# Projections placed evenly over the pairs, and VectorE's emptying of a PSUM item bank moved behind the product of its pair

## Chip, core and metric

One NeuronCore of a Trainium2 chip runs the whole program. The metric is device time in microseconds, the median of three runs. Engines: TensorE (PE), VectorE (DVE), ScalarE (ACT), GpSimd (POOL), and SyncE (SP), whose queue issues every DMA of this kernel.

## What is computed

Input x is (2, 2048, 512). In short:

```python
h = x @ cond_W[id] + cond_b[id]                 # per batch element
q, k, v = split(h @ w_qkv.T)                    # 16 heads of 32
s = causal(q @ k.T / sqrt(32) - slope*|i-j|)
p = 0.5 * (1 + s * rsqrt(1 + s*s));  p /= sum(p) + 1e-6
x1 = x + (p @ v) @ w_out.T
z = layernorm(x1 + relu(x1 @ W1[l] + b1) @ W2[l] + b2) * gamma + beta
out = x1 + int8_linear(z, w8)                   # one scale over all of z
```

The softmax is a rational one: no maximum is taken, and each score s becomes 1 + s/sqrt(1+s²) by elementwise passes.

## The kernel before

**Groups, chunks, pairs.** Attention is done for four heads at a time: 2 batch elements by 4 head groups are 8 groups, G = 0 to 7. A group walks over four chunks c of 512 queries, and within a chunk over the key blocks. Its unit of work is a *pair*: 128 keys by up to 2 x 512 scores, in one of two PSUM slots of `sc`. A group has 68 pairs; chunks begin at pairs 0, 5, 18 and 39 (`first`), and the last five pairs of each chunk lie on the diagonal, with masks added by further small matmuls (L920).

**What a pair costs each engine.** PE makes the scores (L917). ACT squares them (L748), takes the reciprocal root (L750), and later squares 1+g for pair k-2 (L713). DVE multiplies scores and root, the *product* (L1135, `s_g`), and then adds for pair k-2, the *numerator* (L1066, `s_num`). POOL squares y (L674). PE's matmul for pair k+2 needs the slot that the product of pair k frees. Six pairs later PE multiplies the results with v and with ones (L896, the *pv* step, into `ov` and `dn`, for two pairs at a time). At a chunk's last pv step DVE empties `ov` and `dn` (L1079 and L1080; L1180 and L1181 for a chunk of the group before), SP moves the denominators (L532), DVE inverts them (L1084), SP moves them back (L538, L540), and DVE multiplies (L1090, the *divide*). The next chunk's first pv step waits for the emptying (`s_out`).

**Items.** All other PE work is cut into *items* of one or four parts, put between the matmuls of pairs. An item writes one of two banks of `it` and is then emptied, so item i waits until item i-2 has been emptied, and some wait for their own inputs as well (`needs`). Kinds: the projections q, k, v of a chunk of 512 tokens, four parts each (L817, and L821 for v); `xt` and `h`, the conditional linear layer of 128 tokens (L801, L834); `o`, `rt`, `a`, `w2`, `zt`, the output projection, adapter and norm of 128 tokens (L841, L801, L848, L850, L801). DVE empties q, k (L993 and L995, through `stage`), v (L985), xt (L998), h (L1001), o (L1005) and w2 (L1008); ACT empties rt, a and zt. A projection's name with "next" belongs to the group after.

**Who runs items.** Group 0 (`opening`) has projections and 12 tiles of xt and h; groups 1, 2, 5, 6 (`plain`) have 12 projections and nothing else; group 3 (`closing`) adds 16 tiles of xt and h for batch element 1; group 4 (`joining`) adds 16 tiles of o to zt; group 7 (`ending`) has 10 of those and no next group.

**What sets the order.** `Group.__init__` (L108) writes out one list of events, which every engine's program follows: "qk" for pair k, then item parts, then "pv". It keeps a budget `left`, which grows by 1.61 us + `slack` for each pair and shrinks by the cost of a part (0.86 for a projection part). A job may begin from pair `start`, goes at once at pair `end` whatever the budget, and waits `lag` pairs behind the jobs it follows. In DVE's program (`group`, L1092) the product and numerator of pair k are written by `scored(k)`. Before the change that call is held back until the next "pv" or "qk":

```python
for e in g.events:
    if e[0] in ("qk", "pv") and k is not None:
        scored(k)
        k = None
    if e[0] == "qk":
        k = e[1]
    elif e[0] == "item":
        ... empty_item(...)
```

so an item that ends in pair k is emptied in front of the product of pair k, whenever PE has made it.

**SP's order.** For each q or k item SP waits for the emptying and issues 13 DMAs (`operand`, L473 twelve times and L474), which bring the chunk's rows of `stage` to `qmv` or `kst`. PE waits for them (`s_op`) before the chunk's first scores. The queue is one line: the denominators (L532) and the loads of x tiles (L461, L465) stand in it by the event list. At the start of `closing` SP waits until *all* items of the group before have been emptied (`sp.wait_ge(s_evac, dve_base)`), then issues the conditional weights (L478, L480) and two x tiles (L461). At the start of `joining` and `ending` it waits likewise and then issues seven loads of weights (L484) and two x tiles (L465). In `closing` the first xt item stands at pair 2 and waits for its x tile; in `joining` the first o item stands at pair 1 and waits for all seven loads (`s_bw`).

Before the change q of chunk 1 is an item at pair 0 of its own group; v and k of chunk 1 are both items of pair 61 of the group before.

## Time and profile before

| | |
|---|---|
| median of 3 runs | 2234.24 us (2229.65 to 2236.6) |
| the profiled execution: its own time | 2231.39 us |
| its span in the profile | 2229.5 us |
| granted TensorE clock, mean | 0.922 of full |
| busy: PE, DVE, ACT, POOL | 1768.5, 1805.8, 1713.3, 1691.9 us (79, 81, 77, 76% of the span) |
| DVE product L1135, numerator L1066 | 544 each; 662.4 and 773.9 us |
| ACT L748, L750, L713 | 544 each; 551.6, 575.5, 566.2 us |
| ACT idle before L748, of it until PE sc L917 | 310.8 us, 185.6 us |
| DMA | 138.49 MB, mean 62 GB/s |

Busy times are unions of an engine's instructions. The idle time of a group is that of its engine just before those instructions, with what ended it. Four engines lie within five points of each other, so shares don't tell what bounds; the order of waits does. The profiled execution is 2.9 us under the median; a profile covers one execution, so sums are made against its 2231.39 us.

### The profile page before, as it was taken

Reading aid. Unit: us, or ns where it says so; the run is one execution under the profiler, and the core shown is the slowest. Engines: PE = TensorE matmul, PEld = TensorE weight load, DVE = VectorE, ACT = ScalarE, POOL = GpSimd, SP = SyncE. Lnnn points to the kernel's source line nnn. Section 1 sums busy time; section 2 is a strip of 40 time slices with the busy share of each in tenths; the row PEclk is TensorE's granted clock in tenths of the full one; section 3 lists DMA queues with packets and bytes.
Section 4 is the critical chain, followed back from the end, with each engine's and each line's share of the span. In section 5 each row is a group of like instructions: output and inputs, shape, how many; then the busy total and the mean of one; then the engine's idle time right before and its main releaser. Section 6 shows DMA issues by size and latency. Waiting matters only on the chain.

```text
span 2229.5 us, 29232 instructions
## 1 busy us (share of the span) xinstructions
PE 1768.5 (79%) x10640; PEld 897.9 (40%) x10640; DVE 1805.8 (81%) x1730; ACT 1713.3 (77%) x1842; POOL 1691.9 (76%) x720
## 2 busy tenths in 40 slices
PE   5668877777787789999987888886887687897765
PEld 4554433333333336565443443332333233443331
DVE  4238888988889889889785878888889888998838
ACT  0037998889888988878775878898889888897652
POOL 2027888888888887778775877888888888897738
PEclk9899989988988899999998998998999899999889
DMA  5411101110111022211323121210112012222146
GB/s 179 148 49 45 49 21 45 40 49 20 45 41 49 21 68 74 68 34 40 97 63 92 43 77 40 50 54 16 35 47 58 15 46 76 52 61 60 46 165 207
DMA packets 126602, 138.49 MB, mean 62 GB/s; under 512 B 27868, under 2 KB 78044, under 8 KB 126044
## 3 DMA queue, kind: packets, MB, share of 16 engines
q1 hardware_dynamic: 126460, 136.64, 21.6%
q8 instruction: 84, 1.38, 0.3%
q14 instruction: 58, 0.48, 0.1%
HBM read 54.02 MB, written 22.80 MB: 34 GB/s over the span
## 4 chain that ended last, share of the span: by engine, by line
PE 38%; DVE 21%; ACT 21%; issue 11%; POOL 4%; SPq 3%; DMA 2%; DVEq 0%; POOLq 0%; ACTq 0%
ACT yb L748 8%; DVE gb L1135 7%; DVE gb L1066 7%; PE sc L917 7%; ACT gb L713 6%; PE it L817 6%; PE ov L896 6%; ACT yb L750 5%; PE dn L896 5%; PE it L834 4%; PE it L841 3%; PE it L821 3%; SPq L473 3%; POOL oT L707 2%; DMA area<-in_x_dram 1%
## 5 line engine op out<-in xcount | busy, mean ns | idle before, releaser
L674 POOL TENSOR_TENSOR yb<-yb 128x1024 f32<-128x1024 f32 x544 | 1503.0, 2776 | 432.6 <-DVE gb L1135 415.0
L748 ACT ACTIVATE yb<-sc 128x1024 f32<-128x1024 f32 x544 | 551.6, 1014 | 310.8 <-PE sc L917 185.6
L1135 DVE TENSOR_TENSOR gb<-sc,yb 128x1024 f32<-128x1024 f32 x544 | 662.4, 1218 | 142.8 <-ACT yb L750 139.1
L1066 DVE TENSOR_TENSOR gb<-gb,yb 128x1024 f32<-128x1024 f32 x544 | 773.9, 1423 | 0.1
L917 PE MATMUL sc<-qmv,kst 128*128 128x512 f32 (+3 forms) x1280 | 482.8, 461 | 263.0 <-DVE gb L1135 250.5
L750 ACT ACTIVATE yb<-yb 128x1024 f32<-128x1024 f32 x544 | 575.5, 1058 | 17.2
L713 ACT ACTIVATE gb<-gb 128x1024 f32<-128x1024 f32 x544 | 566.2, 1041 | 0.0
L917 PEld LDWEIGHTS sc<-qmv,kst 128*128 128x128 f32 x1280 | 231.5, 202 | 568.1 <-DVE gb L1135 412.0
L896 PE MATMUL ov<-gb,vv 128*32 128x512 f32 (+3 forms) x2560 | 326.4, 594 | 29.5 <-DVE den L1080 24.6
L896 PE MATMUL dn<-gb,ones 128*32 128x512 f32 (+3 forms) x2560 | 312.5, 572 | 0.0
L817 PE MATMUL it<-hT,wT 128*128 128x512 f32 x496 | 245.2, 627 | 8.2 <-ACT area L728 3.2
L896 PEld LDWEIGHTS dn<-gb,ones 128*32 128x32 f32 x2560 | 88.7, 119 | 178.1 <-issue 172.6
L834 PE MATMUL it<-area 128*128 128x128 f32 x1024 | 134.4, 291 | 26.6 <-DVE area L998 22.8
L834 PEld LDWEIGHTS it<-area 128*128 128x128 f32 x1024 | 131.0, 206 | 34.0 <-DVE area L998 27.1
L817 PEld LDWEIGHTS it<-hT,wT 128*128 128x128 f32 x496 | 98.5, 202 | 95.6 <-issue 77.6
L841 PE MATMUL it<-area,oT 128*128 128x512 f32 x224 | 115.0, 646 | 15.6 <-DVE oT L1090 7.4
L821 PE MATMUL it<-wT,hT 128*128 128x128 f32 x992 | 123.1, 278 | 0.7 <-DVE hT L1001 0.5
L821 PEld LDWEIGHTS it<-wT,hT 128*128 128x128 f32 x992 | 120.4, 194 | 6.2 <-DVE area L1008 1.0
L896 PEld LDWEIGHTS ov<-gb,vv 128*32 128x32 f32 x2560 | 56.1, 113 | 156.5 <-issue 96.5
L920 PE MATMUL sc<-unseen,ident 128*128 128x128 bf16 x512 | 116.5, 238 | 0.0
L993 DVE TENSOR_SCALAR stage<-it 128x512 fp32r<-128x512 f32 x64 | 43.6, 681 | 63.6 <-PE it L817 50.5
L801 PE MATMUL it<-ident,area 128*128 128x128 f32 x336 | 53.4, 292 | 43.0 <-POOL area L665 14.4
(113 smaller groups left out, 1086.9 us busy)
## 6 DMA issues: line engine op xcount, KB each, us to landing
qmv<-stage SPq DMA_DIRECT2D x384, 64.0 KB
kst<-stage SPq DMA_DIRECT2D x384, 64.0 KB
area<-in_x_dram SPq DMA_DIRECT2D x58, 256.0 KB, 2.8
out_dram<-oT SPq DMA_DIRECT2D x32, 256.0 KB, 3.2
den<-rec_d SPq DMA_DIRECT2D x31, 256.0 KB
wT<-wT_d SPq DMA_DIRECT2D x7, 768.0 KB, 4.4
x_d<-area SPq DMA_DIRECT2D x16, 256.0 KB, 2.6
z_d<-area SPq DMA_DIRECT2D x16, 256.0 KB, 2.7
```

The source lines that it names most:

```text
L674: pool.tensor_tensor(y, y, y, ALU.mult).then_inc(s_y2, 1)
L713: act.activation(gview(n), gview(n), ACT.Square, bias=1.0).then_inc(s_g2, 1)
L748: act.activation(yview(n), sc[:, n % SLOTS], ACT.Square).then_inc(s_s2, 1)
L750: act.activation(yview(n), yview(n), ACT.Abs_reciprocal_sqrt, bias=1.0).then_inc(s_y, 1)
L817: r = pe.matmul(bank, wT[:, "qk".index(what), part, :], hT[:, part, c * CH:(c + 1) * CH], **ends)
L821: r = pe.matmul(bank[:, part * P:(part + 1) * P], hT[:, k, tok], wT[:, 2, k, :], start=(k == 0), stop=(k == KC - 1))
L834: r = pe.matmul(bank[:, part * P:(part + 1) * P], wc[:, k, part * P:(part + 1) * P], xT[:, a, k, :], start=(k == 0), stop=(k == KC - 1))
L841: r = pe.matmul(bank, oT[:, part, tok], woT[:, part, :], **ends)
L896: r = pe.matmul(dst[p.head * D:(p.head + 1) * D, p.q0:p.q0 + p.width], lhsT, gview(n)[:, p.bank, p.at:p.at + p.width], start=(p.kb == 0), ...
L917: r = pe.matmul(out, kst[:, p.head, p.kb * P:(p.kb + 1) * P], qmv[:, c % 2, p.head, p.q0:p.q0 + p.width], start=True, stop=not diagonal)
L1066: dve.tensor_tensor(gview(n), gview(n), yview(n), ALU.add).then_inc(s_num, 1)
L1135: dve.tensor_tensor(gview(n), sc[:, n % SLOTS], yview(n), ALU.mult).then_inc(s_g, 1)
```

## The change

It does five things. (1) The list of projections is written out with a start and an end for each; q of chunk 1 becomes an item of the group before (`("q", 1, "next")`, from pair 63, placed between pairs 64 and 67), and k and v of chunk 1 are no longer in one pair. (2) The budget of a pair becomes 0.9 + slack, with every group's own slack raised by 0.7, so that it stays the same in the four other groups and falls from 1.61 to 0.9 in `plain`. (3) DVE writes `scored(k)` at the "qk" event, so an item that ends in pair k is emptied behind product, numerator, inversion and divide of pair k. (4) SP waits for the group's last scores before it issues the 13 DMAs of the moved q, since they overwrite the slot of `qmv` that chunk 3 uses. (5) The numbering of banks and the waits for them are carried over the border of groups, since the number of items is odd in some.

```diff
--- before.py
+++ after.py
@@ -138,22 +138,21 @@
                 made.setdefault((job.name[1] // TT, 0 in chunks), []).append(job)
-        projections = []
-        for c in range(n_chunks):
-            p0, p1 = self.first[c], self.last[c]
-            if c < n_chunks - 1:
-                whats = "qkv" if c or opens else "q"
-                for what in whats:
-                    lag = 0 if what == "q" or c == 0 else STAGED
-                    after = [] if what == "q" else [projections[-1]] if what == "k" else []
-                    projections.append(Job((what, c + 1), [0.86] * 4, made.get((c + 1, False), []) + after,
-                                           p0 + (2 if c else 0), p1 - (6 if c else 4) + (4 if what == "v" else 0), lag or EVAC))
-            elif has_next:
-                for what, nxt, start in (("q", 0, 2), ("v", 0, 2 * TT + LAG), ("k", 0, 2 * TT + 2),
-                                         ("v", 1, 4 * TT + LAG), ("k", 1, 4 * TT + 2)):
-                    after = [projections[-2]] if what == "k" else []
-                    projections.append(Job((what, nxt, "next"), [0.86] * 4, made.get((nxt, True), []) + after,
-                                           p0 + start, p1 - 6, STAGED if what == "k" else EVAC))
+        f, end = self.first, len(self.pairs) - 1
+        over = [f[3] + 2 * TT * (c + 1) for c in range(2)]
+        wanted = [(("q", 1), 0, 0), (("k", 1), 0, 8), (("v", 1), 0, 13)] if opens else []
+        wanted += [(("q", 2), f[1] + 1, f[2] - 5), (("k", 2), f[1] + 2, f[2] + 8), (("v", 2), f[1] + 3, f[2] + 10),
+                   (("q", 3), f[2] + 1, f[3] - 5), (("k", 3), f[2] + 2, f[3] - 3), (("v", 3), f[2] + 3, f[3])]
+        if has_next:
+            wanted += [(("q", 0, "next"), f[3] + 1, f[3] + 16), (("k", 0, "next"), over[0] + 1, end - 8),
+                       (("v", 0, "next"), over[0] + LAG, end - 6), (("k", 1, "next"), over[1] + 1, end - 4),
+                       (("v", 1, "next"), over[1] + LAG, end - 2), (("q", 1, "next"), end - 4, end)]
+        projections, staged = [], None
+        for name, start, until in wanted:
+            after = made.get((name[1], len(name) == 3), []) + ([staged] if name[0] != "v" and staged else [])
+            projections.append(Job(name, [0.86] * 4, after, start, until, EVAC if name[0] == "v" or not staged else STAGED))
+            if name[0] != "v":
+                staged = projections[-1]
         tracks = [[job for job in others if job.name[1] % 2 == 0], [job for job in others if job.name[1] % 2], projections]
         self.events, current, part, left, order = [], None, 0, 0.0, []
         n_pairs, n_units = len(self.pairs), len(self.units)
@@ -165,7 +164,7 @@
         for k in range(n_pairs):
             self.events.append(("qk", k))
-            left = max(-1.0, min(left, 0.5)) + 6 * CH / 1200 - 0.95 + slack
+            left = max(-1.0, min(left, 0.5)) + 0.9 + slack
             while True:
                 if current is None:
                     ready = [t for t in tracks if t and t[0].start <= k and
@@ -193,7 +192,6 @@
         self.items = [job for job in order if job.parts]
         self.operands = [job.name for job in self.items if job.name[0] in ("q", "k")]
         self.ranks, self.evacs = ranks(self.items)
-        assert not has_next or len(self.items) % BANKS == 0 and all(eng == "dve" for eng, _ in self.ranks[-BANKS:])
     def item(self, *name):
         return [job.name for job in self.items].index(name)
@@ -216,10 +214,10 @@
     first = plain.first + [len(plain.pairs)]
     opening = Group(NC, [job for j in range(TT, KB)
-                         for job in cond_jobs(j, first[j // TT - 1], first[j // TT] - (12 if j >= 2 * TT else 5))], True, True, 0.8)
+                         for job in cond_jobs(j, first[j // TT - 1], first[j // TT] - (12 if j >= 2 * TT else 5))], True, True, 1.5)
     closing = Group(NC, [job for j in range(KB)
-                         for job in cond_jobs(j, 2 if j < TT else first[j // TT] + 1, first[NC] - 24 + j)], True, slack=0.0)
+                         for job in cond_jobs(j, 2 if j < TT else first[j // TT] + 1, first[NC] - 24 + j)], True, slack=0.7)
     def joined(j):
@@ -228,12 +226,12 @@
         return after_jobs(j, 1 if c < NC - 1 else LAG + 10, min(over - 3 if i < 2 else over, first[NC] - 1),
                           min(over - 1 if i < 2 else over + 8, first[NC] - 1))
-    joining = Group(NC, [job for j in range(KB) for job in joined(j)], True, slack=0.8)
+    joining = Group(NC, [job for j in range(KB) for job in joined(j)], True, slack=1.5)
     assert all(job.at <= first[job.name[1] // TT + 1] + LAG - 2 for job in joining.items if job.name[0] == "o")
     DONE = KB - TT - 2
     ending = Group(NC, [job for j in range(DONE) for job in
-                        after_jobs(j, first[j // TT + 1] + LAG + 2 * NORM_LAG + 3, first[NC] - 9 + j - KB + TT, first[NC] - 1)], False, slack=0.3)
+                        after_jobs(j, first[j // TT + 1] + LAG + 2 * NORM_LAG + 3, first[NC] - 9 + j - KB + TT, first[NC] - 1)], False, slack=1.0)
     UNITS, PAIRS = len(plain.units), len(plain.pairs)
     TOTAL = B * NG * PAIRS
@@ -447,7 +445,7 @@
         def ops_before(g, G):
-            return 2 if g is opening else 2 * NC * G + 3
+            return 2 if g is opening else 2 * NC * G + 4
         def zs_before(b, j):
@@ -588,6 +586,8 @@
                     if what in ("q", "k"):
                         sp.wait_ge(s_evac, dve_base + rank)
                         nhg = hg if len(e[1].name) == 2 else (0 if g is closing else hg + 1)
+                        if e[1].name == ("q", 1, "next"):
+                            sp.wait_ge(s_qk, (G + 1) * PAIRS)
                         operand("qk".index(what), c, nhg)
                     elif what == "v" and c == NC - 1 and g.has_next:
                         sp.wait_ge(s_item, base + item + 1)
@@ -781,10 +781,12 @@
         def _(pe):
             pe.wait_ge(s_const, 2)
-            def emptied(i, of, dve_base, act_base):
-
-                if i < 0:
+            def emptied(i, of, dve_base, act_base, before=None):
+
+                if i < 0 and before is None:
                     pe.wait_ge(s_evac, dve_base + i + 1)
+                elif i < 0:
+                    emptied(len(before.items) + i, before.ranks, dve_base - before.evacs["dve"], act_base - before.evacs["act"])
                 elif of[i][0] == "dve":
                     pe.wait_ge(s_evac, dve_base + of[i][1])
                 else:
@@ -909,7 +911,7 @@
                             pe.wait_ge(s_g, n - SLOTS + 1)
                         for what, at in (("q", g.first[c]), ("k", g.first[c] + 2 * TT * c)):
                             if k == at:
-                                own = g.operands.index((what, c)) + 1 if (what, c) in g.operands else -(c == 0 and carry)
+                                own = g.operands.index((what, c)) + 1 if (what, c) in g.operands else -2 * (c == 0 and carry)
                                 pe.wait_ge(s_op, 16 * NPROJ * (ops_before(g, G) + own))
                         for p in g.pairs[k]:
                             out = slot[:, p.bank, p.at:p.at + p.width]
@@ -922,10 +924,10 @@
                     elif e[0] == "part":
                         d = b + (1 if g is closing else -1 if g is joining else 0)
                         if e[2] == 0:
-                            emptied(item - BANKS, g.ranks, dve_base, act_base)
+                            emptied(item - BANKS, g.ranks, dve_base, act_base, before[0])
                             if g is opening and e[1].name == ("q", 1):
                                 pe.wait_ge(s_wt, 16)
-                        r = compute(it[:, (PRO + item) % BANKS], e[1], e[2], d, G + 1 if len(e[1].name) == 3 else G,
+                        r = compute(it[:, (base + item) % BANKS], e[1], e[2], d, G + 1 if len(e[1].name) == 3 else G,
                                     g.ranks, dve_base, act_base)
                     elif e[0] == "item":
                         r.then_inc(s_item, 1)
@@ -941,8 +943,10 @@
                             own = c >= 2 or c and not carry
                             pe.wait_ge(s_evac, dve_base + (g.ranks[g.item("v", c)][1] if own else 0))
                         products(G, g, u)
+                before[0] = g
             pe.wait_ge(s_const, 9)
+            before = [None]
             for_groups(group)
             for u in plain.late:
                 products(B * NG, plain, u)
@@ -1115,7 +1119,7 @@
                     if len(name) == 3:
                         v_free = G * UNITS + units_over(c)
                         k_free = G * PAIRS + pairs_over(c)
-                        q_free = G * PAIRS + last
+                        q_free = G * PAIRS + last if c == 0 else None
                     elif what in ("q", "k", "v"):
                         if carry:
                             v_free = (G - 1) * UNITS + units_over(c)
@@ -1124,7 +1128,7 @@
                             q_free = G * PAIRS + g.first[c - 1]
                         elif carry:
                             q_free = G * PAIRS
-                    empty(name, d, base + item, dve_base + g.ranks[item][1], ops_before(g, G) + his, v_free, q_free, k_free, (PRO + item) % BANKS)
+                    empty(name, d, base + item, dve_base + g.ranks[item][1], ops_before(g, G) + his, v_free, q_free, k_free, (base + item) % BANKS)
                 def scored(k):
@@ -1146,11 +1150,9 @@
                 k = None
                 for e in g.events:
-                    if e[0] in ("qk", "pv") and k is not None:
-                        scored(k)
-                        k = None
                     if e[0] == "qk":
                         k = e[1]
+                        scored(k)
                     elif e[0] == "item":
                         eng, rank = g.ranks[item]
                         if eng == "dve":
@@ -1169,8 +1171,6 @@
                                 output(G, hg, g, u, c, g is opening and c == 0)
                             else:
                                 output_prev(G, prev_hg, u, c)
-                if k is not None:
-                    scored(k)
                 for late in reduced:
                     largest(*late[1:])
```

## Rows read from the trace of the kernel before

**Rows 1.** Busy time by stretch: groups 2, 3, 4, 7 and 0

```profile
core 0: us, PE busy (x) PEld busy (x) DVE busy (x) ACT busy (x) POOL busy (x), PEclk, DMA share, GB/s
...
600.30:825.70 225.40, 176.11 (x1057) 77.87 (x1056) 198.18 (x173) 200.50 (x206) 191.56 (x69) 0.90 0.17 45
825.70:1066.50 240.80, 225.59 (x1635) 142.27 (x1634) 213.60 (x205) 202.21 (x205) 191.43 (x69) 0.98 0.22 61
1066.50:1395.00 328.50, 273.71 (x1470) 136.79 (x1469) 248.06 (x269) 238.13 (x301) 238.19 (x133) 0.93 0.23 63
...
1846.20:2102.50 256.30, 213.87 (x1253) 100.73 (x1251) 227.01 (x226) 223.06 (x266) 220.23 (x109) 0.94 0.18 50
91.00:375.20 284.20, 225.08 (x1448) 134.19 (x1447) 205.47 (x191) 200.41 (x203) 186.49 (x67) 0.93 0.16 41
```

**Rows 2.** Timeline, two pairs of group 2 with no items

```profile
729.84 1.23 DVE L1135 TENSOR_TENSOR gb<-sc,yb 128x1024 f32<-128x1024 f32 x1 [0.59 <-ACT yb L750]
730.59 1.00 ACT L748 ACTIVATE yb<-sc 128x1024 f32<-128x1024 f32 x1
730.98 1.22 DVE L1066 TENSOR_TENSOR gb<-gb,yb 128x1024 f32<-128x1024 f32 x1
...
731.12 0.74 PE L917 MATMUL sc<-qmv,kst 128*128 128x512 f32 x2 [0.36 <-DVE gb L1135]
...
733.54 1.00 ACT L748 ACTIVATE yb<-sc 128x1024 f32<-128x1024 f32 x1
```

**Rows 3.** Timeline, DVE and ACT, pairs 0 and 1 of group 2

```profile
602.36 0.69 DVE L993 TENSOR_SCALAR stage<-it 128x512 fp32r<-128x512 f32 x1 [0.43 <-PE it L817]
...
605.14 1.02 ACT L748 ACTIVATE yb<-sc 128x1024 f32<-128x1024 f32 x1 [1.77 <-PE sc L920]
```

**Rows 4.** Timeline, PE, DVE and ACT, pair 61 of group 2

```profile
802.64 3.60 PE L817 MATMUL it<-hT,wT 128*128 128x512 f32 x8
...
806.28 0.69 DVE L993 TENSOR_SCALAR stage<-it 128x512 fp32r<-128x512 f32 x1 [2.74 <-PE it L817]
...
806.81 1.02 ACT L748 ACTIVATE yb<-sc 128x1024 f32<-128x1024 f32 x1 [2.85 <-PE sc L917]
```

**Rows 5.** Timeline, PE, pair 20 of group 2

```profile
665.97 3.27 PE L817 MATMUL it<-hT,wT 128*128 128x512 f32 x4
```

**Rows 6.** Timeline, PE and ACT, pair 12 of group 2

```profile
642.14 1.93 PE L896 MATMUL ov<-gb,vv 128*32 128x512 f32 x8 [2.71 <-DVE den L1080]
...
646.36 1.02 ACT L748 ACTIVATE yb<-sc 128x1024 f32<-128x1024 f32 x1 [4.50 <-PE sc L920]
```

**Rows 7.** Timeline, SP and DVE, pairs 25 to 29 of group 2

```profile
687.78 7.48 SPq L473 DMA_DIRECT2D kst<-stage  x12
...
698.47 0.25 DVE L1084 RECIPROCAL rec<-rec 128x16 f32<-128x16 f32 x1 [2.76 <-DMA rec<-den]
```

**Rows 8.** Timeline, PE, ACT: group 0 pair 20; group 3 pair 43

```profile
215.21 3.47 PE L834 MATMUL it<-area 128*128 128x128 f32 x16 [3.80 <-DVE hT L1001]
...
221.30 1.02 ACT L748 ACTIVATE yb<-sc 128x1024 f32<-128x1024 f32 x1 [8.05 <-PE sc L917]
...
987.23 1.02 ACT L748 ACTIVATE yb<-sc 128x1024 f32<-128x1024 f32 x1 [4.71 <-PE sc L917]
```

**Rows 9.** Timeline, SP, ends of groups 2 and 3

```profile
815.95 0.44 SPq L478 DMA_DIRECT2D area<-in_L_cond_W_dram  x1
...
817.03 1.29 SPq L461 DMA_DIRECT2D area<-in_x_dram  x2
...
1056.68 0.35 SPq L484 DMA_DIRECT2D area<-woT_d  x1
...
1060.49 0.38 SPq L484 DMA_DIRECT2D bet<-in_L_cond_beta_dram  x1
```

**Rows 10.** DMA issues: KB each, median us from issue to landing

```profile
area<-in_x_dram SPq DMA_DIRECT2D x58, 256.0 KB, 2.8
...
area<-in_L_cond_W_dram SPq DMA_DIRECT2D x2, 1024.0 KB, 5.5
```

## The prediction, made before the change was run

> **What bounds the kernel now.** The four engines' busy shares are too close to name one, so I first read busy time by stretch, a stretch being a group from its first L748 to the next group's [rows 1]. A plain group lasts 225.4 us and ACT is busy for 200.5 of it; closing lasts 240.8, joining 328.5, ending 256.3, opening 284.2, while ACT's work hardly grows (202 in closing) and PE's does (226 and 274). Then I read the timeline where a plain group has no items: one square (L748) starts 2.95 us after the other, with no idle time on ACT, while DVE waits 0.59 before each product and PE waits for the slot [rows 2]. So undisturbed pairs are bound by ACT, 68 x 2.95 = 200.6 us a group, and a plain group loses 24.8 us to stalls. That the reader is to see: time is lost only where ACT waits before L748, nearly always because PE brought the scores late.
>
> In group 2 three of these waits are large. After pair 0, PE is in four parts of q: ACT idles 1.77 [rows 3]. In pair 61, v and k together: PE computes k until 806.2, DVE stands 2.74 before emptying it, ACT idles 2.85 [rows 4]. At pair 12, DVE is late with emptying `ov` and `dn` (a divide is in front), PE waits 2.71 for it, then its pv matmuls run slowly, ACT idles 4.50 [rows 6]. The other 24.8 - 1.8 - 2.9 - 4.6 = 15.5 us are shorter waits of the same kinds, one of them behind a 2.76 us wait of DVE for denominators, whose L532 stands in SP's queue behind the 13 DMAs of k3 [rows 7].
>
> **Where the items go.** I followed the planner's arithmetic (budget, starts, ends, lags) for both versions. In plain, items that took two pairs take three (2, 1, 1 parts), k1 is at pairs 56 to 59, v1 at 61 to 63, q1 at 64 to 67. In the other groups the budget is the same, and mostly the projections' places change. I counted how often an item needs a bank or an input that DVE empties from an item of the same pair or the one before. Plain: never, in either version. Same pair: closing 2 before, 3 after; joining 7 and 12; ending 1 and 0; opening, without pair 0, 7 and 8. Pair before: about 70 in both.
>
> **Term 1, plain groups, four times.** Gone: pair 0 (1.8) and pair 61 (2.9) [rows 3, 4]. The inversion's wait: k3 now ends at pair 26, behind SP's L532 of that pair, not before it; of 2.76 us on DVE some 1.1 reached ACT, since product and numerator (1.14 us each by their starts [rows 2]) leave 0.59 + the PE's lead. Two projection parts with a pv step took PE too long where the clock was low: 3.27 us for four matmuls, where eight took 3.60 [rows 4, 5]; one part there saves about 0.6 at four places, 2.4. Returned: the diagonal pairs 63 to 67 now hold six parts at 0.9 (a quarter of 3.60), with about 1 us uncovered. Pair 12 stays: the divide and `s_out` are not touched. Emptying behind the numerator holds up the next product by 2 x 1.14 + 1.4 - 2.95 = 0.7, under the PE's lead, which is 733.54 - 731.12 - 0.74 = 1.7; if the clock is low that cover is 1.2. Sum 1.8 + 2.9 + 1.1 + 2.4 - 1 = 7.2, times 4: **-29** (bounds -12: pairs 0 and 61 alone, with what the tail gives back; -52: half of the 24.8).
>
> **Term 2, SP's queue at two borders.** The moved q is the last item, and its 13 DMAs now stand in front of the next group's loads; the loads also wait for its emptying. Closing: emptying ends some 3.5 us after the first square, as now [rows 3]; 13 DMAs take 8.0 (7.48 and one of about 0.5 [rows 7]); the x tile is issued 1.1 after the weights [rows 9] and lands in 2.8 [rows 10]: 3.5 + 8.0 + 1.1 + 2.8 = 15.4. PE stands at xt of pair 2 until then, then has two xt (1.1), a pv step in low clock (3.2), scores (1.2): square 3 at 20.9, not 3 x 2.95 = 8.9: +12. Now these loads go out at 816 to 818 [rows 9], 8 us before the group. Joining: emptying ends near the first square (the item is at pair 66), 8.0, 3.8 from first to last weight [rows 9], landing 5.5 (the median of a weight tile [rows 10]) = 17.5; o needs all seven; three parts (4) and scores (1.2) put square 2 at 22.7 where two pairs and the q gave 7: +16. Ending needs its weights at pair 20: covered. SP's new wait for the group's last scores costs nothing: they are issued before the item's emptying ends. The moved q's own DMAs land at 3.5 + 8.0 + 2.8 = 14.3 after the first square in plain, and pair 5's scores are wanted near 5 x 2.95 - 0.8 = 13.9; that is where the same 13 DMAs land now, so again nothing. Together **+28** (20 to 32).
> The page DMA: Bandwidth & Descriptors of the Trainium skill (Rules for kernel authors) says to issue a DMA early and wait late; the change does the reverse here, and no row prices that other than as above.
>
> **Term 3, waits for a bank inside a pair or from the pair before.** An item that ended in pair k was emptied as soon as PE was done. Now the emptying waits for scores (0.74), square and root (2.0), product and numerator (2.3): some 5 us after the pair's scores start, 6 with its own 0.7, while PE reaches the dependent item after 2. PE executes in order, so pv of k and scores of k+1 stand behind it. Before has two places where an emptying was late like this: behind a numerator and a divide PE waited 3.80 and ACT then idled 8.05; behind a numerator alone ACT idled 4.71 [rows 8]. A same-pair need thus costs between 0 (PE far ahead) and 8; I take 4, nearer to the row without a divide. There are 17 such pairs (the chain in opening's pair 6 counted once): 68, less 25 for waits those places have already. The other side of this edit is that a product no longer stands behind an unfinished item; in pairs 0 and 61 of plain that is in term 1, and in closing and joining PE is by then behind with the next scores, so the earlier product frees a slot, and a square of POOL's, that nobody waits for yet: nothing, at best some of the 25 us. A need from the pair before is mostly covered by a pv step: 0 to 2, I take 0.5, some 50 times: 25. **+68** (5 to 142).
>
> **Term 4, pairs 0 and 61 in the others.** Pair 0 three times 1.8, pair 61 three times 2.9, less 1 for each tail: **-12** (-15 to -9). In opening's pair 0 the first xt is emptied 6 us later (root and product of pair 0 come first), and k1 leaves the chain, worth as much: 0. **Term 5:** in closing, joining and ending k3 stays ahead of L532 and is emptied 2.3 later, so DVE waits longer for the inversion: **+3** (0 to 6).
>
> Sum: -29 + 28 + 68 - 12 + 3 = **+58**, against the profiled execution's 2231.4 (span 2229.5 and 1.9 around it): 2289; the median of the runs lies 2.9 higher, so 2292.
>
> **Rivals.**
> *A, the two banks cover it.* If PE is far enough ahead, term 3 is near 0 and -29 + 28 - 12 + 3 leaves -10: 2224. It decides where term 3 stays under 4. For it: PE is idle 20% in plain. Against: it is busy for 226 of 240.8 us in closing [rows 1]. The Trainium skill's page Perfetto Trace Analysis (Matmuls) has independent matmul groups rotate through PSUM banks so that emptying one overlaps the next one's matmuls; by it this rival would win.
> *B, the clock.* Spread parts leave PE less busy at a stretch, and plain is already at 0.90 [rows 1]. A part at low clock is 3.27 / 2 - 3.60 / 4 = 0.73 dearer [rows 4, 5]; 48 parts, a third of it uncovered, 12 us a group: 58 + 48, 2340. Against: closing is at 0.98 with spread items.
> The same page (Matmul Optimizations) says that it matters that matmuls run back to back in batches; the rows of low clock here follow PE's waits, as it would have it.
> *C, plain gains almost nothing*, as the tail on the diagonal gives back pairs 0 and 61 and the rest is `s_out`: term 1 is -5: 2316.
> *D, the terms cancel:* 2235.
>
> **Chances.** Forecast 0.50, A 0.20, B 0.10, C 0.12, D 0.08. 0.3% (6.7 us) is about what a measurement can tell from no change. Faster 0.20, same 0.08, slower 0.72. The range: term 3 alone gives 2229 to 2366 with the others kept; I cut it to 2220 to 2350, which takes in A, B, C and D and leaves out the ends of two terms together.
>
> **What would show it.** Right: plain stretches near 218; in closing ACT idle some 12 us before square 3, with PE waiting for area<-in_x_dram, in joining 16 before square 2; PE's waits for DVE's emptying lines (L998, L1001, L1005, L993, L1008) grow by tens of us in sum. L1084 no longer waits in plain. Wrong: if PE's waits for emptied banks don't grow, A holds; if the granted clock in plain falls below 0.88, B. A plain group above 222 is C. If closing and joining start without a wait for DMA, term 2 fails.

## The result and the profile after

| | before | after |
|---|---|---|
| median | 2234.47 us (4 runs, 2229.65 to 2236.6) | 2396.72 us (4 runs, 2388.09 to 2398.59) |
| profiled execution: own time, span | 2231.39, 2229.5 us | 2398.59, 2396.7 us |
| granted clock, mean | 0.922 | 0.893 |

The ratio is 1.0724, with an interval of 1.0704 to 1.0744. The kernel became slower by 162 us. The prediction said slower, by 58, in a range that ended at 2350: the sign is right, the size is not, and the result lies outside the range.

The first view is busy time by stretch, of the kernel after: groups 1, 2 (both plain), 3 (closing), 4 (joining), 7 (ending) and 0 (opening), the stretches of [rows 1] and one plain group more:

```profile
core 0: us, PE busy (x) PEld busy (x) DVE busy (x) ACT busy (x) POOL busy (x), PEclk, DMA share, GB/s
387.90:603.80 215.90, 173.17 (x1060) 76.73 (x1056) 196.60 (x171) 200.03 (x206) 191.57 (x69) 0.92 0.15 39
603.80:819.00 215.20, 171.85 (x1060) 75.84 (x1056) 199.24 (x173) 200.09 (x206) 191.64 (x69) 0.93 0.16 40
819.00:1107.20 288.20, 235.84 (x1636) 146.78 (x1632) 211.84 (x207) 202.28 (x206) 191.48 (x69) 0.91 0.18 49
1107.20:1541.40 434.20, 306.41 (x1472) 155.12 (x1472) 237.61 (x269) 240.02 (x301) 221.26 (x132) 0.83 0.19 54
...
1972.60:2269.70 297.10, 225.54 (x1236) 105.11 (x1232) 221.45 (x226) 224.35 (x266) 213.70 (x109) 0.89 0.18 51
91.90:387.90 296.00, 235.30 (x1468) 138.84 (x1468) 200.74 (x194) 200.76 (x204) 186.12 (x67) 0.90 0.15 40
```

A plain group takes 215 to 216 us where it took 225.4, and its clock rose from 0.90 to 0.93. Everything else grew: opening by 11.8, closing by 47.4, joining by 105.7, ending by 40.8 us. ACT's and DVE's work in these stretches is what it was to within 12 us. In joining PE's busy time rose from 273.7 to 306.4 us for the same work (1470 and 1472 matmuls recorded), at a granted clock of 0.83 in place of 0.93.

Where the time stands idle, from the costliest groups of instructions of the page after:

```profile
L1139 DVE TENSOR_TENSOR gb<-sc,yb 128x1024 f32<-128x1024 f32 x544 | 663.0, 1219 | 436.2 <-ACT yb L750 433.3
L748 ACT ACTIVATE yb<-sc 128x1024 f32<-128x1024 f32 x544 | 550.7, 1012 | 445.0 <-PE sc L919 248.1
```

ACT's idle time before the square grew from 310.8 to 445.0 us, DVE's before the product from 142.8 to 436.2. DVE waits for ACT's root, ACT for PE's scores; what PE waits for closes the ring. PE's rows in the view of waits after:

```profile
PE sc L919 <- DVE gb L1139: 202.0, 169, 4.8
PE it L836 <- DVE area L1002: 36.5, 11, 11.3
...
PE it L803 <- DMA area<-in_x_dram: 26.7, 4, 12.4
...
PE it L843 <- DVE area L1009: 19.9, 5, 5.0
PE it L803 <- DVE hT L1005: 18.5, 6, 6.0
PE it L850 <- DVE area L1009: 15.6, 7, 4.2
PE it L803 <- DVE vv L989: 14.7, 4, 7.5
```

The columns are the sum, the number of waits and the longest. The first row is PE's wait for a slot of `sc`; it was 250.5 us before, so it is not what grew. Summed over all rows of this view in which PE waits for one of DVE's emptying lines, it is 51.5 us in 35 waits before and 181.9 us in 62 waits after.

Lengths of all groups, from a group's first L748 to the next group's (ending: to 3.4 us behind its own last), in us; worked out from the starts of L748 in each trace. The kernels below the first two are the experiments that follow.

| kernel | opening | plain | plain | closing | joining | plain | plain | ending |
|---|---|---|---|---|---|---|---|---|
| before | 284.2 | 225.1 | 225.3 | 240.9 | 328.5 | 225.9 | 225.3 | 256.3 |
| after | 296.0 | 215.9 | 215.2 | 288.2 | 434.2 | 216.0 | 215.2 | 297.1 |
| after, emptying in front again | 277.5 | 215.0 | 215.2 | 251.1 | 361.7 | 216.1 | 215.5 | 258.5 |
| before, emptying behind | 303.4 | 230.3 | 231.1 | 286.2 | 387.3 | 231.1 | 229.7 | 304.2 |
| after, loads first | 295.1 | 215.9 | 215.2 | 274.6 | 424.0 | 215.9 | 215.4 | 300.3 |
| after, emptying between | 298.9 | 222.1 | 225.6 | 277.8 | 401.1 | 223.3 | 225.3 | 275.3 |
| front and loads first | 275.6 | 215.1 | 215.2 | 239.9 | 348.8 | 213.1 | 214.8 | 259.3 |

### The profile page after: what moved, and what is told of

Same layout as the page of the kernel before. It is cut to its first block, busy times and chain, and to the rows that moved or that the text cites. A ratio compares the mean times of both kernels' runs of the same rounds, so it can differ in the third digit from the quotient of the medians.

```text
span 2396.7 us, 29236 instructions
## 1 busy us (share of the span) xinstructions
PE 1819.2 (76%) x10637; PEld 924.9 (39%) x10640; DVE 1781.9 (74%) x1730; ACT 1715.3 (72%) x1842; POOL 1668.4 (70%) x720
## 3 DMA queue, kind: packets, MB, share of 16 engines
q1 hardware_dynamic: 126460, 136.64, 20.3%
## 4 chain that ended last, share of the span: by engine, by line
PE 33%; ACT 27%; DVE 17%; issue 10%; POOL 6%; SPq 3%; DMA 3%; DVEq 0%; POOLq 0%; ACTq 0%
ACT yb L748 11%; ACT yb L750 8%; ACT gb L713 8%; DVE gb L1070 6%; PE sc L919 6%; PE ov L898 6%; DVE gb L1139 5%; PE dn L898 5%; PE it L843 4%; PE it L836 4%; PE it L819 4%; POOL yb L674 3%; SPq L471 3%; POOL oT L707 2%; PE it L823 1%
## 5 line engine op out<-in xcount | busy, mean ns | idle before, releaser
L674 POOL TENSOR_TENSOR yb<-yb 128x1024 f32<-128x1024 f32 x544 | 1494.6, 2759 | 495.1 <-DVE gb L1139 479.3
L1139 DVE TENSOR_TENSOR gb<-sc,yb 128x1024 f32<-128x1024 f32 x544 | 663.0, 1219 | 436.2 <-ACT yb L750 433.3
L748 ACT ACTIVATE yb<-sc 128x1024 f32<-128x1024 f32 x544 | 550.7, 1012 | 445.0 <-PE sc L919 248.1
L1070 DVE TENSOR_TENSOR gb<-gb,yb 128x1024 f32<-128x1024 f32 x544 | 758.2, 1394 | 3.6 <-POOL yb L674 3.6
L919 PE MATMUL sc<-qmv,kst 128*128 128x512 f32 (+3 forms) x1280 | 489.3, 467 | 215.2 <-DVE gb L1139 202.0
L750 ACT ACTIVATE yb<-yb 128x1024 f32<-128x1024 f32 x544 | 575.5, 1058 | 17.3
L898 PE MATMUL ov<-gb,vv 128*32 128x512 f32 (+3 forms) x2560 | 334.0, 607 | 35.6 <-DVE den L1084 27.9
L819 PE MATMUL it<-hT,wT 128*128 128x512 f32 x496 | 257.7, 630 | 19.3 <-DVE area L1012 6.7
L843 PE MATMUL it<-area,oT 128*128 128x512 f32 x224 | 130.9, 720 | 64.3 <-DVE area L1009 19.9
L836 PEld LDWEIGHTS it<-area 128*128 128x128 f32 x1024 | 136.2, 212 | 49.1 <-DVE area L1002 40.4
L803 PE MATMUL it<-ident,area 128*128 128x128 f32 x336 | 60.7, 317 | 97.4 <-DMA area<-in_x_dram 26.7
L823 PE MATMUL it<-wT,hT 128*128 128x128 f32 x992 | 129.0, 279 | 7.2 <-DVE area L1012 7.2
L843 PEld LDWEIGHTS it<-area,oT 128*128 128x128 f32 x224 | 48.5, 228 | 111.0 <-issue 63.8
```

The source lines that it names most:

```text
L674: pool.tensor_tensor(y, y, y, ALU.mult).then_inc(s_y2, 1)
L748: act.activation(yview(n), sc[:, n % SLOTS], ACT.Square).then_inc(s_s2, 1)
L750: act.activation(yview(n), yview(n), ACT.Abs_reciprocal_sqrt, bias=1.0).then_inc(s_y, 1)
L819: r = pe.matmul(bank, wT[:, "qk".index(what), part, :], hT[:, part, c * CH:(c + 1) * CH], **ends)
L823: r = pe.matmul(bank[:, part * P:(part + 1) * P], hT[:, k, tok], wT[:, 2, k, :], start=(k == 0), stop=(k == KC - 1))
L836: r = pe.matmul(bank[:, part * P:(part + 1) * P], wc[:, k, part * P:(part + 1) * P], xT[:, a, k, :], start=(k == 0), stop=(k == KC - 1))
```

## The experiments

The first four ran on one chip, beside a median before of 2232.58 us (12 runs). Theory W says that the loss is the emptying behind product and numerator; P, that the projections' new places cost it.

**1. The new places, the old order.** DVE empties the items of a pair in front of its product again:

```
                 for e in g.events:
+                    if e[0] in ("qk", "pv") and k is not None:
+                        scored(k)
+                        k = None
                     if e[0] == "qk":
                         k = e[1]
-                        scored(k)
...
+                if k is not None:
+                    scored(k)
```

> The changed kernel with one edit undone: DVE empties an item in front of the product of its pair again; placement, budgets and the moved q stay. Theory W (the waits behind the product are the loss): plain groups keep most of their gain (216 to 219 us each), closing falls from 288 to near 250, joining from 434 to near 335, ending from 297 to near 255, opening from 296 to near 282; the waits for loads at the start of closing and joining (15 and 16 us) stay, so 2225 us, between 2205 and 2250. Rival P (the new places of the items are the loss, with more needs inside one pair): the run stays above 2330.

Measured: 2228.07 us (9 runs), ratio 0.9975 (0.9960 to 0.9990). The whole loss is gone, so W stands and P falls. (Joining came out at 361.7 us, where near 335 was expected; experiments 3, 5 and 9 are about that.) Taken away from the kernel after, the order is worth 168.6 us. The plain groups keep their 215 to 216 us: there the order costs nothing. PE's waits for DVE's emptying fall to 63.1 us in 31 waits, 119 less than after.

Pair 46 of closing shows the mechanism. It ends h of tile 11 and has two xt items, so the second xt needs the bank that h filled. The kernel after, timeline of PE, ACT and DVE (start, length, engine, line, idle before and what ended it):

```profile
1020.03 0.60 PE L803 MATMUL it<-ident,area 128*128 128x128 f32 x4
1026.59 1.11 PE L803 MATMUL it<-ident,area 128*128 128x128 f32 x4 [5.95 <-DVE hT L1005]
1027.63 1.94 PE L898 MATMUL ov<-gb,vv 128*32 128x512 f32 x8
1029.34 1.93 PE L898 MATMUL dn<-gb,ones 128*32 128x512 f32 x8
1031.20 1.22 PE L919 MATMUL sc<-qmv,kst 128*128 128x512 f32 x2
...
1032.52 1.02 ACT L748 ACTIVATE yb<-sc 128x1024 f32<-128x1024 f32 x1 [9.36 <-PE sc L919]
...
1023.01 1.22 DVE L1139 TENSOR_TENSOR gb<-sc,yb 128x1024 f32<-128x1024 f32 x1
1024.15 1.78 DVE L1070 TENSOR_TENSOR gb<-gb,yb 128x1024 f32<-128x1024 f32 x1
1025.85 0.68 DVE L1005 TENSOR_TENSOR hT<-it,cbias 128x512 f32<-128x512 f32 x1
```

And the same pair with the old order:

```profile
972.56 0.60 PE L803 MATMUL it<-ident,area 128*128 128x128 f32 x4
975.50 1.11 PE L803 MATMUL it<-ident,area 128*128 128x128 f32 x4 [2.35 <-DVE hT L1005]
...
979.57 0.73 PE L919 MATMUL sc<-qmv,kst 128*128 128x512 f32 x2
...
980.39 1.02 ACT L748 ACTIVATE yb<-sc 128x1024 f32<-128x1024 f32 x1 [4.71 <-PE sc L919]
...
974.77 0.68 DVE L1005 TENSOR_TENSOR hT<-it,cbias 128x512 f32<-128x512 f32 x1
```

DVE begins to empty h 5.8 us behind the start of PE's first xt, where it was 2.2. PE stands 5.95 us where it stood 2.35, in order, with `pv` and the next scores behind. Then those run slowly too: from the second xt to the end of the scores PE needs 5.8 us, where it needed 4.8. So ACT idles 9.36 us where it idled 4.71: 3.6 from the wait, 1 from slower matmuls.

Taken over all pairs outside the plain groups, kernel after less this one: the 18 pairs in which an item waits for an item of its own pair cost 56 us (3.1 each), the 48 in which one waits for an item of the pair before 82 us (1.7 each), the others 29 us.

The mean of 1.7 hides two kinds. Of the 48 pairs, 35 have a pv step between the item waited for and the one that waits: they cost 32 us together, 0.9 each, and 19 of them differ by at most half a us. The other 13 have none, and cost 50 us, 3.9 each. Closing's pair 33 is the dearest of these: `h` of tile 7 needs the `xt` of pair 32, and pair 32 has no pv step. The kernel after:

```profile
966.45 2.38 DVE L1094 TENSOR_TENSOR oT<-oT,den 128x512 f32<-128x512 f32 x1
968.75 1.28 DVE L1002 COPY area<-it 128x512 f32<-128x512 f32 x2
...
969.58 3.76 PE L836 MATMUL it<-area 128*128 128x128 f32 x16 [5.56 <-DVE area L1002]
```

And with the old order:

```profile
927.43 1.27 DVE L1002 COPY area<-it 128x512 f32<-128x512 f32 x2
...
928.26 2.02 PE L836 MATMUL it<-area 128*128 128x128 f32 x16 [0.44 <-DVE area L1002]
```

Here the emptying stood behind a divide (L1094) too. PE waited 5.56 us for it, and the same 16 matmuls then took 3.76 us in place of 2.02.

**2. The old places, the new order**: experiment 1's edit the other way, in the kernel before.

> The kernel before with this one edit: DVE empties an item behind product and numerator of its pair; placement, budgets and SP's order are those of before. Theory W: plain within 5 us of 225 each, joining and ending dearer by about 70 and 40 us, closing by 30, opening by 10: 2380 us, between 2340 and 2420. Rival P: below 2270.

Measured: 2425.89 us, ratio 1.0862 (1.0835 to 1.0888): 193 us, just above the range expected (2340 to 2420). The surprise is in the plain groups, which lose 5 us each with the order alone, while with the new places it costs them nothing. The places of the change thus cover part of what its order costs. Outside the plain groups it costs 19, 45, 59 and 48 us, where with the new places it costs 19, 37, 73 and 39 (the table's second row less its third). The 5 us have a place in the trace: DVE's waits for `rec<-den` before the inversion L1084 are 16.8 us in the two plain groups 1 and 2, where they were 6.4, and the largest is at pair 29, which takes 7.9 us for 4.1 in group 2:

```profile
728.30 0.25 DVE L1084 RECIPROCAL rec<-rec 128x16 f32<-128x16 f32 x1 [5.36 <-DMA rec<-den]
```

k of chunk 3 is emptied later, so its 13 DMAs go out later, and the denominators stand behind them in SP's queue. In the kernel after no inversion of a plain group waits.

**3. The next group's loads first.** In the kernel after, SP is made to issue the weights and first x tiles of the next group before the 13 DMAs of the moved q, not behind them (the weights of joining and ending move in the same way):

```
...
-                if g is closing:
-                    sp.wait_ge(s_evac, dve_base)
-                    cond_weights(b + 1, cids[b + 1])
-                    for j in range(2):
-                        load_x(b + 1, j)
...
+                        if e[1].name == ("q", 1, "next"):
+                            sp.wait_ge(s_evac, dve_base + rank - 1)
+                            next_loads()
```

> The changed kernel, but SP issues the next group's weights and first tiles ahead of the 13 DMAs of the moved q (after the emptying of the item before it), not behind them. If the late loads cost what their pairs show (pair 2 of closing 18.2 us, pair 1 of joining 19.0, where 2.95 is undisturbed), both pairs fall below 5 us and the run takes 31 us less, 2366 (2355 to 2375). Rival: the time is taken elsewhere, since PE must then wait for something else in those pairs or for the q operand at pair 5: less than 10 us gained.

Measured: 2372.47 us, ratio 1.0612 (1.0587 to 1.0637): 24.3 us less than after, under the 31 expected but within the range. In the kernel after, SP's queue and PE at closing's start (group starts at 819.0):

```profile
821.92 7.47 SPq L471 DMA_DIRECT2D qmv<-stage  x12
829.43 0.48 SPq L472 DMA_DIRECT2D qmv<-qal  x1
830.11 0.43 SPq L476 DMA_DIRECT2D area<-in_L_cond_W_dram  x1
...
836.69 1.94 PE L803 MATMUL it<-ident,area 128*128 128x128 f32 x8 [12.41 <-DMA area<-in_x_dram]
```

With the loads first, SP's queue there (the group starts at 817.4):

```profile
808.22 0.43 SPq L476 DMA_DIRECT2D area<-in_L_cond_W_dram  x1
808.84 0.41 SPq L478 DMA_DIRECT2D cbias<-in_L_cond_b_dram  x1
809.29 1.26 SPq L459 DMA_DIRECT2D area<-in_x_dram  x2
820.32 8.63 SPq L471 DMA_DIRECT2D qmv<-stage  x12
```

From closing's first square to its fourth it is 10.9 us, where it was 24.1. Closing gains 13.6 us and joining 10.2.

**4. Emptying between product and numerator**, in the kernel after: `scored(k)` keeps the product; numerator and the rest of a pair come in a second function behind the items.

> The changed kernel with the emptying between product and numerator: 1.14 us earlier by the starts of these two. Theory W, with the price of a dependent item falling with that latency at some 35 to 45 places: 35 to 50 us less, 2355 (2335 to 2370). Rival: what counts is that the product's own wait for the root comes first, and the numerator is hidden: within 10 us of 2397. If the later numerator holds up ACT's squares, plain groups get slower than 216 us.

Measured: 2371.59 us, ratio 1.0619 (1.0585 to 1.0653): 25 us less than after, where 35 to 50 were expected. Joining, ending and closing gain 33, 22 and 10 us, since items are emptied 1.1 us earlier; the plain groups lose 6 to 10 us each. What they lose is in the waits of ACT, whose square waits for an earlier numerator. The row of the kernel after, and, behind it, that of this one:

```profile
ACT yb L748 <- DVE gb L1070: 7.2, 9, 1.6
```

```profile
ACT yb L748 <- DVE gb L1070: 72.4, 79, 3.9
```

So both orders have a price: late emptying stops PE, a late numerator stops ACT.

Experiments 5 to 8 ran beside a median before of 2234.04 us (9 runs).

**5. Edits 1 and 3 together**: the new places, the old order, and the loads first.

> The changed kernel with both repairs: items emptied in front of the product again (e1) and the next group's loads issued ahead of the moved q's DMAs (e3). If the two are independent, 2228.1 less the 24.3 that e3 took off: 2204, between 2198 and 2212, 1.3% under the kernel before, and faster than both kernels. Rival: with the early emptying the late loads were partly hidden, so less than 12 us off.

Measured: 2203.28 us (5 runs), ratio 0.9854 (0.9834 to 0.9873). This beats both kernels. Its stretches of plain, closing, joining and ending:

```profile
582.40:797.60 215.20, 172.15 (x1060) 76.61 (x1056) 200.30 (x174) 199.72 (x205) 192.22 (x69) 0.93 0.18 47
797.60:1037.60 240.00, 224.03 (x1636) 141.85 (x1632) 211.62 (x206) 202.39 (x206) 191.83 (x69) 0.98 0.23 62
1037.60:1386.40 348.80, 277.46 (x1472) 141.16 (x1472) 245.04 (x269) 238.36 (x302) 236.83 (x132) 0.92 0.22 60
1814.30:2073.60 259.30, 209.98 (x1236) 98.87 (x1232) 227.41 (x225) 222.75 (x266) 220.84 (x109) 0.94 0.18 49
```

Against [rows 1] a plain group is 10 us shorter, closing and its clock are as before, joining is still 20 us longer.

**6, 7. In front only where a need is near.** The order is chosen pair by pair: an item is emptied in front of the product if an item begun in the same pair waits for it (6), or one begun in the same pair or the next (7), and so are the items ahead of it in its pair; the others are emptied behind. Of the edit in the kernel after:

```
+                k, pending, front = None, False, g.front(REACH)
...
+                    if pending and (e[0] in ("qk", "pv") or e[0] == "item" and item > front.get(k, -1)):
                         scored(k)
+                        pending = False
```

> The changed kernel, but items are emptied in front of the product of their pair where an item begun in the same pair waits for them (and the items before them in that pair); all others behind. By pair, the changed kernel and e1 differ by 56 us in the 18 pairs with such a need outside plain groups, by 82 us in 48 pairs that need an item of the pair before, by 29 us elsewhere. If the need itself is the cause, 50 to 60 us less than 2396.7: 2341 (2325 to 2355). Rival (how many items are emptied late counts, not who needs them): about 20 us less.

> As e6, and in front also where an item begun in the next pair waits for it. If needs over one pair carry the 82 us: 2396.7 - 56 - 82 = 2259 (2235 to 2275); whatever is left above the 2228 of e1 is then not bound to a need. Plain groups have no such needs and keep the emptying behind. Rival: 2330 or more, little below e6.

Measured: 2344.7 us, ratio 1.0501 (1.0478 to 1.0524), and 2255.8 us, ratio 1.0100 (1.0085 to 1.0116). In shares of the kernel before, the change's order costs 7.5% (1.0724 less 0.9975); 2.2 points come from items needed in their own pair, 4.0 from those needed in the next. In us that is 50 and 90, close to the 56 and 82 counted by pair in experiment 1.

**8. POOL's square first.** In the kernels before and after alike, POOL's square L674 of a pair stands behind POOL's own steps of that pair (`b2` and `norm`, which wait for DVE); here it is put in front of them.

> The changed kernel, with POOL's square of pair k put in front of POOL's steps of that pair (b2 and norm), where it stood behind them. POOL waited 94.6 us before L660 for DVE's L1018 in the changed kernel, 21.0 before. If this queue is part of the loss (squares late, so numerators and ACT's squares late), 20 to 30 us less. If the loss is PE waiting for banks and inputs alone, within 10 us of 2397, or slower, since the norm then starts up to 2.8 us later.

Measured: 2388.52 us, ratio 1.0687 (1.0669 to 1.0704): 8 us less than after. POOL's queue is at most a small part.

**9, 10. Which places cost joining its 20 us?** From kernel 5, the projections get their places of the kernel before, q of chunk 1 excepted: in joining alone (9), and in all four groups that are not plain (10). They ran beside a median before of 2234.55 us.

> e5, with the projections of joining alone at the places of the kernel before (q of chunk 1 stays in the group before, and the next group's is at pairs 63 to 67). Joining took 348.8 us in e5 and 328.5 before; pairs with a need inside themselves fall from 11 to 6, and x tiles are again requested ahead of the first o emptying. If the new places are what costs joining the 20 us, it comes back to 325 to 332 and the run to 2185 (2178 to 2192). Rival (the 20 us belong to the moved q or to TensorE's clock): within 6 us of 2203.

> e5, with the old places in opening, closing, joining and ending, the new ones in plain alone. Closing 239.9 in e5 and 240.8 before, ending 259.3 and 256.3, opening 275.6 and 284.2: if only joining's places matter, within 8 us of e9; closing loses 3 as pair 61 holds two projections again, opening too, ending gains 3.

Measured: 2205.73 us, ratio 0.9864 (0.9838 to 0.9890), and 2220.04 us, ratio 0.9940 (0.9919 to 0.9961). The first is a miss: joining stays at 354.7 us, and the new places within it are not what lengthens it. Against before, the excess of kernel 9 lies in pairs 0 to 11 (65.0 us for 57.4) and 12 to 22 (84.1 for 68.5), and later pairs differ by 3 us. In kernel 5 the largest excess is pair 9, 17.4 us for 8.6:

```profile
1072.14 7.56 SPq L471 DMA_DIRECT2D qmv<-stage  x12
1080.28 0.35 SPq L463 DMA_DIRECT2D area<-in_x_dram  x1
...
1083.23 0.69 DVE L1011 TENSOR_TENSOR area<-it,area 128x512 f32<-128x512 f32 x1 [6.63 <-DMA area<-in_x_dram]
...
1091.80 1.02 ACT L750 ACTIVATE yb<-sc 128x1024 f32<-128x1024 f32 x1 [12.97 <-PE sc L921]
```

The x tile that the emptying of an `o` adds to goes out behind the DMAs of a q; DVE stands at it, PE waits 9.17 us for that emptying, and ACT idles 12.97. In kernel 9 the longest such wait is another: DVE stands 11.04 us at the emptying of k for the DMAs of q (`qmv<-qal`), at pair 11. So SP's queue has a part in it. How much of the 20 us is not shown: in the kernel before, DVE waits 19.5 us for x tiles in joining too, against 22.4 in kernel 5.

The second is a miss too: 14 us above kernel 9, where at most 8 was expected. In it, opening and closing are 12 and 8 us longer than in kernel 5 and ending 8 shorter: the new places help the first two and cost in ending. And though all projections but one stand where they stood, the four groups together are 31 us longer than before, 26 of them in joining. What they still share with kernel 5 is the moved q, with the loads issued at it and the items behind it shifted.

**11. The reach of experiment 7 put to two pairs.** It ran beside a median before of 2231.91 us.

> e7 with the reach set to two pairs: in front also where an item begun two pairs later waits. e7 stands 28 us above e1 (2255.8 and 2228.1). If those are needs over two pairs (a w2 emptying whose norm POOL and then zt wait for, above all), 20 to 28 us less: 2232 (2225 to 2240). If they are emptyings that nobody waits for soon, within 6 us of 2256.

Measured: 2245.64 us (6 runs), ratio 1.0054 (1.0037 to 1.0070). Against 7 it gains half a point, 10 us, where 20 to 28 were expected or, by the rival, at most 6. Some 0.8 points, 18 us, remain between it and kernel 1, in which everything is emptied in front: they belong to emptyings that no item waits for within two pairs, and what waits for them was not found.

## Why the prediction was right and wrong

**The bound** was right in the main: undisturbed pairs follow each other by 2.95 us after as before, ACT's own work did not grow, and over the eight groups its idle time grew by 164 us (345.9 to 510.1). But "only where ACT waits before L748" was too narrow: 134 us of it lie there, and 30 lie before ACT's own emptyings of items (L731, L728, L725), which wait for PE too.

**Term 1**, plain groups, -29 predicted: -39.3 measured (901.6 us for the four before, 862.3 after), inside its bounds of -12 to -52. Pairs 0 and 61 now take 2.95 us as forecast, pair 12 stayed (7.5). Undersized were the short waits: pairs 20, 27 and 41, 4.0 to 4.3 us long before, take 2.95, and the diagonal, pairs 62 to 67, gave nothing back (18.35 us, for 18.87 before) where 1 us was taken for it. L1084 no longer waits, as forecast. Rival C falls. The emptying behind the numerator cost plain nothing, as argued, though by a narrower margin than the text had it: with the old places the same order costs 5 us a group (experiment 2), through the wait of the inversion.

**Term 2**, SP's queue, +28 predicted: mechanism and size right. PE waited 12.41 us for area<-in_x_dram, closing's fourth square came 24.1 us after its first, and joining's third 21.9; I had 20.9 and 22.7. Before, they came after 10.7 and 7.0 us, so the two starts lost 28 us. (Two slips are small: joining's 8.0, 3.8 and 5.5 add to 17.3, not 17.5; and its 7 us from before hold pair 0's wait, about 1 us, which term 4 takes off again.) To issue the loads first gave back 24 us with the new order and 25 with the old one (2228.07 to 2203.28). The page DMA: Bandwidth & Descriptors of the Trainium skill (Rules for kernel authors), which wants a DMA issued early and waited for late, is borne out by these two runs.

**Term 3** is the step that failed: "A same-pair need thus costs between 0 (PE far ahead) and 8; I take 4", "less 25 for waits those places have already", "A need from the pair before is mostly covered by a pv step: 0 to 2, I take 0.5". The sum was +68 (5 to 142); the order is worth 168.6 us. Item by item:
- The needs inside a pair added 56 us, 3.1 each, where 68 less 25 = 43 was forecast. The 25 us for waits already there should not have come off: in pair 46 the new delay is laid on the old wait (2.35 to 5.95 us), and does not replace it.
- The needs from the pair before cost 82 us in 48 pairs, where 25 was forecast. This is the largest error. The cover by a pv step is real where there is one: those 35 pairs cost 0.9 us each, near the 0.5. But 13 of the 48 have no pv step between, and they cost 3.9 each, 50 us: more than a need inside a pair. "Mostly covered" was never counted, and no row was given for it. Experiment 7 confirms the sum (90 us), not this division, which is read from two traces.
- 29 us lie in pairs with neither need, which I had at nothing; experiment 11 leaves 18 for emptyings that no item waits for within two pairs, and their mechanism is open.
- Slower matmuls add to a wait. PE's matmuls behind the long waits of pairs 46 and 33 took longer than behind the short ones, and term 3 had no price for that.

**Term 4**, -12 (its own figures add to -11), was right at the pairs it names and wrong for the groups. Pair 0 fell to 2.95 us in closing, joining and ending, pair 61 in opening (3.1), closing and joining: 15 us gained, 14 forecast before the tails. But with order back and loads first (kernel 5) against before, opening gains 8.6 us, closing 1.0, and ending loses 3.0 and joining 20.3, so that the four groups are 14 us longer and not 12 shorter: what the term put at nothing is the rest of joining. That is the second thing that I had not foreseen, and its cause is open but for the waits shown at experiment 9. **Term 5** (+3) is too small to tell apart; its mechanism is the one that experiment 2 shows in plain.

**Rival A** fell, by the 169 us of experiment 1: two banks don't cover the late emptying. The rule of the page Perfetto Trace Analysis of the Trainium skill (Matmuls), that rotating banks lets the emptying of one overlap the matmuls of the next, holds here in the plain groups with the new places, where the order moved 215.0 to 215.9 us at most, and, going by the count above, for most needs with a pv step between. Another page of the Trainium skill, PSUM — Partial Sum Buffer (Summary: rules for kernel authors), asks for prompt evacuation, for the sake of space. In the other four groups the trace agrees with the rule though not with that reason: late emptying cost 56 and 82 us for needs in the same pair and the next, through PE's waits.

**Rival B** was looked for in the wrong place. Plain's clock rose to 0.93. It fell where PE waited: joining 0.93 to 0.83, ending 0.94 to 0.89, closing 0.98 to 0.91. With the order put back it is 0.90, 0.93 and 0.96. That edit changes nothing but the place of DVE's emptying, so the fall of the clock follows from it and is part of its price, not a cause of its own.

Split by runs, the change is: the new places with loads first, 31 us under before (kernel 5; by its trace -43 in plain and +14 elsewhere), the late loads +25, the order +169. That these add to the 162 measured is no test, since each run is taken away from the next; what they give is the share of each. The range failed with it: I "cut it to 2220 to 2350" to leave out the ends of two terms together, while one term alone went past its end of 142.

## What to carry to other kernels

Where an in-order producer (PE) shares few banks among items, the place of an emptying in the consumer's queue is part of the critical path: empty in front of the elementwise chain when an item of the same pair or the next needs the bank or the data, and count those needs before moving it, those without another long step of the producer between them above all. A cover must be counted where the needs are, need by need. And a change with several edits should be split: here the new places and an early issue of the loads are worth 1.5%, and the new order alone costs 7.5%.

## What the runs showed of the hardware

I had not expected the granted clock to fall so far with dependency waits: it fell from 0.90 in joining with the emptying in front to 0.83 with it behind, and PE's busy time for the same 1472 matmuls rose from 280.1 to 306.4 us. It is seen in single rows: the last two score matmuls of pair 46 took 0.73 us with the short wait and 1.22 us behind the long one. So such a wait can be paid twice: once as idle time, and again in slower matmuls.

The 12 DMAs of 64 KB kept SP's queue for 7.47 us in one kernel and 8.63 us in another, some 0.62 to 0.72 us each, which is the length of two pairs and a half for every load that stands behind them.
